# Ranks of the last batch and the second plan moved earlier, low halves ahead of the finish, and four banks for the products of the experts

## The reference

```python
x = x + xattn(layernorm(x), ctx, Wq, Wg, bg, Wkv, Wo)
# the second layer
y = layernorm(x)
w, sel = top_k(y @ Wr, 2); w = softmax(w)          # Wr: 512 x 8
gate = einsum('bsk,bske->bse', w, one_hot(sel, 8))
for e in range(8):
    out = out + gate[..., e:e+1] * (y @ We[e] + be[e])   # We[e]: 512 x 512
x = x + out
```

## Time and profile before

| | |
|---|---|
| median of 3 runs | 540.89 us |
| the profiled execution's own time | 540.51 us |
| its span | 538.5 us |
| TensorE busy | 517.9 us, 96% of the span |
| VectorE busy | 310.1 us |
| GpSimd busy | 213.4 us |
| adds of the second stage | 39, a median of 5.4 us (result buffers `khat`) and 5.5 us (`buf`) from issue to landing |

### The profile page before, as it was taken

How to read it: one execution, slowest core, us unless ns; L and a number is a source line. 1 busy time by engine, 2 the same in 40 slices (tenths; PEclk the granted TensorE clock), 3 DMA queues, 4 the chain that set the end, 5 groups by cost and what they waited for, 6 DMA issues and landing times.

```text
span 538.5 us, 12127 instructions
## 1 busy us (share of the span) xinstructions
PE 517.9 (96%) x4084; PEld 420.6 (78%) x4084; DVE 310.1 (58%) x918; ACT 209.2 (39%) x372; POOL 213.4 (40%) x238
## 2 busy tenths in 40 slices
PE   7999999999999999999999999999999988999992
PEld 4777788888878878887888888788887766888881
DVE  4583348647434773853467386366876777555551
ACT  5455432443433234344323434532253332344430
POOL 4451566412565033146601633100124663445453
PEclk9999999999999999999999999999999998999997
DMA  8922446981445117235420741398979996767765
GB/s 279 392 93 73 163 137 186 265 297 49 154 160 185 50 73 242 80 122 198 139 96 10 265 159 54 130 365 283 365 270 216 219 271 126 163 135 124 158 87 68
DMA packets 41242, 92.94 MB, mean 173 GB/s; under 512 B 5152, under 2 KB 5152, under 8 KB 41056
## 3 DMA queue, kind: packets, MB, share of 16 engines
q0 software_dynamic: 15184, 42.56, 29.9%
q1 hardware_dynamic: 25424, 48.58, 27.0%
q10 hardware_dynamic: 576, 1.05, 0.6%
HBM read 53.81 MB, written 40.18 MB: 175 GB/s over the span
## 4 chain that ended last, share of the span: by engine, by line
PE 78%; DMA 12%; DVE 3%; issue 3%; POOLq 2%; ACT 1%; POOL 0%; SPq 0%; DVEq 0%
PE pj L1173 22%; PE pj L1175 21%; PE pj L1174 21%; PE tp L1165 7%; DMA out_dram<-buf,out_idx 5%; DMA out_dram<-khat,out_idx 5%; PE pj L1260 3%; PE kvb L1232 2%; PE pj L1182 1%; DMA wraw<-in_L_xattn_Wkv_dram 1%; PE tp L1240 1%; POOLq L616 1%; POOLq L617 1%; ACT buf L702 0%; PE kvb L1165 0%
## 5 line engine op out<-in xcount | busy, mean ns | idle before, releaser
L1173 PE MATMUL pj<-R 128*128 128x512 f32 x448 | 183.6, 410 | 0.9 <-DVE R L821 0.9
L1175 PE MATMUL pj<-R 128*128 128x512 f32 x448 | 175.6, 392 | 0.0
L1174 PE MATMUL pj<-R 128*128 128x512 f32 x448 | 174.7, 390 | 0.0
L1173 PEld LDWEIGHTS pj<-R 128*128 128x128 f32 x448 | 84.3, 188 | 19.3 <-DVE R L830 2.2
L1175 PEld LDWEIGHTS pj<-R 128*128 128x128 f32 x448 | 84.1, 188 | 18.9
L1174 PEld LDWEIGHTS pj<-R 128*128 128x128 f32 x448 | 84.5, 189 | 15.0
L1173 PE MATMUL pj<-R,aux 128*128 x156 | 65.2, 418 | 4.9 <-DVE aux L834 3.5
L1175 PE MATMUL pj<-R,aux 128*128 x156 | 62.1, 398 | 0.0
L1174 PE MATMUL pj<-R,aux 128*128 x156 | 61.5, 394 | 0.0
L513 POOL TENSOR_TENSOR rstd<-rstd,mhalf 128x1 f32<-128x1 f32 (+1 forms) x20 | 13.3, 665 | 108.5 <-DVE rstd L848 108.5
L830 DVE TENSOR_TENSOR R<-tp,R 128x512 fp32r<-128x512 f32 x64 | 43.4, 683 | 14.5 <-ACT R L659 14.5
(11 more groups left out here) (197 smaller groups left out, 725.2 us busy)
## 6 DMA issues: line engine op xcount, KB each, us to landing
we_halves<-aux POOLq DMA_DIRECT2D x28, 512.0 KB, 4.7
R<-we_halves SPq DMA_DIRECT2D x28, 512.0 KB, 6.2
buf<-xs SPq DMA_DIRECT2D x39, 264.0 KB, 4.6
buf<-in_ctx_dram SPq DMA_DIRECT2D x15, 512.0 KB, 4.0
wraw<-in_L_ffn_We_dram POOLq DMA_DIRECT2D x14, 512.0 KB, 5.3
wraw<-in_x_dram SPq DMA_DIRECT2D x4, 1024.0 KB, 9.9
out_dram<-gate SPq DMA_DIRECT2D x3, 1024.0 KB, 5.2
xs<-zeros POOLq DMA_DIRECT2D x4, 594.0 KB, 9.1
```

Of the source, the lines that this page charges most:

```text
L1173: nc.tensor.matmul(bank[:, :], s_hi(k), m_hi(k), start=(k == 0), stop=False)
L1174: nc.tensor.matmul(bank[:, :], s_hi(k), m_lo(k), start=False, stop=False)
L1175: last = nc.tensor.matmul(bank[:, :], s_lo(k), m_hi(k), start=False, stop=(k == KT - 1))
```

## The change

1. `START` has L 3 ahead of tile 7 (it was behind it), K 2 behind tile 7 (was behind 8), K 3 behind tile 8 (was behind 10).
2. VectorE and ScalarE walk a second list, `LATE`, made of `START`: from tile 8 on the finish M of tile m stands behind T of tile m + 2. TensorE and GpSimd still walk `START`.
3. The product of tile m from 8 on goes to bank `pj[m % 4]`, and waits for the finish of m - 4 instead of m - 2; tiles 10 and 11 wait for the ranks of quarters 2 and 3 instead.
4. The six pieces of `plan_rest` stand one ahead of each finish of the tiles 9 to 14. The row starts (`tile_row`) are in the fifth piece and raise `planned` to 2, which SyncE waits for as before; the flags for the adds and the row masks are in the sixth and raise it to 3, for which VectorE and GpSimd wait. Three memsets of one element become one of three.

On TensorE, with bank numbers: the rows from the last matmul of tile 6 to the first of tile 7, before. Line 1191 is K 1, line 1182 would be an L, line 1240 the turn of tile 8.

The diff, cut to its core:

```diff
-        START += [("K", "", 1)] + tiles(7) + [("L", "", 3)] + tiles(8) + [("K", "", 2)] + tiles(9) + tiles(10) + [("K", "", 3)]
+        START += [("K", "", 1), ("L", "", 3)] + tiles(7) + [("K", "", 2)] + tiles(8) + [("K", "", 3)] + tiles(9) + tiles(10)
...
+        LATE, due = [], []
+        for place_ in START:
+            if place_[0] == "M" and place_[2] >= 8:
+                due.append(place_)
+                continue
+            LATE.append(place_)
+            if place_[:2] == ("T", "m"):
+                LATE += due
+                due = []
+        LATE += due
+
+        def m_bank(m):
+
+            return pj[m % (2 if m < 8 else 4)]
...
             for step, kind, i in START:
                 if step == "M":
                     if i == M0:
-                        pool.wait_ge(planned, 2)
+                        pool.wait_ge(planned, 3)
...
-            for step, kind, i in START:
+            for n, (step, kind, i) in enumerate(LATE):
                 if step == "T" and kind == "m":
-                    e_of = expert_of(i - 1)
+                    e_of = expert_of(LATE[n + 1][2]) if LATE[n + 1][0] == "M" else None
...
+                link(nc.vector.tensor_tensor(more, big, over(shift_e[:, :], M1), ALU.mult))
+                link(nc.vector.tensor_reduce(tile_o[:, :], more, AX_X, ALU.add))
+                link(nc.vector.tensor_tensor(tile_b[:, :], iota_t[:, :], tile_o[:, :], ALU.add))
+                flag_tiles(ends, bound, big, more, tile_u)
+                link(nc.vector.scalar_tensor_tensor(tile_u, tile_b[:, :], float(P), tile_u, ALU.mult, ALU.min))
+                nc.vector.scalar_tensor_tensor(tile_row[:, M0:M_ALL], tile_e[:, :], float(ROWS), tile_u, ALU.mult, ALU.add).then_inc(planned, 1)
+                yield
...
             planning = plan_rest(bias[:, :])
-            for step, kind, i in START:
+            for step, kind, i in LATE:
                 if step == "T" and kind == "m":
                     low_m(i, i % 2)
                     pay(i)
                 elif step == "M":
-                    if i >= 11:
-                        next(planning, None)
+                    if i >= 9:
                         next(planning, None)
                     copy_y(i)
...
-                pe.wait_ge(MOE["y_copied"], mth(m - 2))
+                if m in (10, 11):
+                    pe.wait_ge(SEMS["ranked"], nth("ranked", LAST, m - 8))
+                else:
+                    pe.wait_ge(MOE["y_copied"], mth(m - (2 if m < 10 else 4)))
...
-                three(pj[slot], lambda k: xsT_hi[:, slot, k, :], lambda k: xsT_lo[:, slot, k, :],
+                three(m_bank(m), lambda k: xsT_hi[:, slot, k, :], lambda k: xsT_lo[:, slot, k, :],
```

More of the change, by code:

```diff
@@ L791, in _ @@
                 elif step == "M":
-                    if i == M_ALL - 1:
-                        e_of = expert_of(i)
-                    gate_bias(i, e_of)
+                    gate_bias(i, expert_of(i) if e_of is None else e_of)
+                    e_of = None
                 elif step == "L":
@@ L1074, in plan_rest @@
                 halves_at(tmp, HALVES - 1, bound, last[:, 1:1 + E])
-                for zero in (last, flag, ends):
-                    link(nc.vector.memset(zero[:, 0:1], 0.0))
+                firsts = tmp[:, at + 3 * M1 + 2 * (E + 1):at + 3 * M1 + 5 * (E + 1)].rearrange("p (a e) -> p a e", a=3)
+                link(nc.vector.memset(firsts[:, :, 0:1], 0.0))
                 link(nc.vector.tensor_tensor(first, first, last[:, 0:E], ALU.is_ge))
@@ L1089, in plan_rest @@
                 yield
+                link(nc.vector.tensor_tensor(more, big, over(shift_e[:, :], M1), ALU.mult))
[5 more added lines that the diff above has]
+                yield
+                link(nc.vector.scalar_tensor_tensor(tile_o, tile_b[:, :], float(P), tile_u, ALU.mult, ALU.subtract))
+                nc.vector.scalar_tensor_tensor(taken[:, :], tile_o, lane[:, 0:1], zeros[:, TOKEN:TOKEN + 1].broadcast_to((P, M1)), ALU.is_gt, ALU.mult)
                 flag_tiles(flag, bound, big, more, tile_u)
@@ L1093, in plan_rest @@
                 nc.vector.tensor_tensor(tile_alone[:, M0:M_ALL], tile_u, offs[:, 2:3].broadcast_to((P, M1)), ALU.mult)
[L1094 to L1105, removed]
+                nc.vector.scalar_tensor_tensor(tile_early[:, M0:M_ALL], tile_t[:, :], 1.0, offs[:, 2:3].broadcast_to((P, M1)), ALU.is_le, ALU.mult).then_inc(planned, 1)
+                dve.wait_ge(planned, 3)
             dve.wait_ge(zeroed, 1)
@@ L1123, in copy_y @@
                 dve.wait_ge(bias_gated, m + 1)
-                nc.vector.scalar_tensor_tensor(y_sb[m % YS], pj[m % 2][:, :], w_sel[:, m % (2 * YS):m % (2 * YS) + 1], y_sb[m % YS],
+                nc.vector.scalar_tensor_tensor(y_sb[m % YS], m_bank(m)[:, :], w_sel[:, m % (2 * YS):m % (2 * YS) + 1], y_sb[m % YS],
                                                ALU.mult, ALU.add).then_inc(MOE["y_copied"], 1)
             planning = plan_rest(bias[:, :])
-            for step, kind, i in START:
+            for step, kind, i in LATE:
                 if step == "T" and kind == "m":
```

## The result

The changed kernel takes 543.68 us (median of 11 runs, 540.13 to 546.34) against 540.86 us (11 runs, 539.81 to 543.58) before: a ratio of 1.0043, interval 1.0023 to 1.0063. Two more sets of runs, each on a chip shared with its own runs of before, gave 1.0029 (1.0004 to 1.0055) and 1.0034 (1.0014 to 1.0053). So the change is slower, by 1.6 to 2.3 us by these ratios (the medians differ by 1.4 to 2.8). The forecast was 541.4, the range 539.0 to 543.6.

What follows compares the result with a forecast made beforehand. TensorE's time and GpSimd's queue of adds, close together, were taken to bound the kernel. The 540.51 us of before plus 0.85 for the later add of tile 30 gave 541.4 us; range 539.0 to 543.6.

Steps and rivals of the forecast that it cites:

- What bounds: Whole kernel: TensorE's time and GpSimd's queue of adds bound it, close together; TensorE's gains count only as adds follow.
- the chain at the end is still made of adds: Expected sign at the end of the run: the last chain of waits goes from add to add.
- an end of the adds that moves with TensorE: Sign at the end of the run that would show the forecast wrong.
- Ranks earlier: TensorE ahead of L 3: it waits for the ranks of quarter 1, so tile 11 turns 1.2 us later.
- The second plan: VectorE's planning pieces around tiles 11 to 14: row starts written at 448.15, only 1.6 us earlier than before.
- The wait in its place and the clock: TensorE ahead of tile 17: waits 3.3 to 4.5 us for the load, then loses 1.6 to low clock.
- The finish is later for the adds: VectorE at tile 30: its finish ends at 505.5 behind tile 32's low half, so add 30 is issued 0.85 us later.
- Other tiles before 30 have more room: GpSimd's adds before tile 30 wait for landings, not finishes, so later finishes were given no cost there.
- Rival A: Longer pause at tile 17 brings more than one half-clock stretch; tile 18 turns at 459.2; 543.0 us, chance 0.26.
- B: The clock holds through the pause at tile 17; TensorE gains 2.1 us; 539.8 us, chance 0.16.
- C: Tile 17's load comes early enough, TensorE stays dense and adds alone bound; 538.8 us, chance 0.08.
- D: Going round four banks with small pauses makes the clock fall repeatedly, costing 14 us; 555 us, chance 0.01.

Runs made afterwards that it cites:

- control 1: The changed kernel run again with no edit, on the chip of three of the experiments: 542.90 us, ratio 1.0029 to the kernel before.
- control 2: The changed kernel run once more with no edit, on the chip of three other experiments: 543.73 us, ratio 1.0034 to the kernel before.

## Why the prediction was right or wrong

**What bounds.** Right in that there are two bounds close together, and the runs without adds put 4.2 us on the adds. But "the chain at the end is still made of adds" holds in full for one of the three profiles of the changed kernel. In the other two the chain stays on TensorE to 518.8 and to 504.6, as "an end of the adds that moves with TensorE" would have it, which the prediction called a sign of being wrong.

**Ranks earlier.** Right. 1.12 us of pause ahead of L 3 came, and tile 11 turned 1.2 to 1.3 us later from tile 0 where I took 1.2.

**The second plan.** Right in place, too early in time. `tile_row` was forecast at 448.15, and came at 448.49 in a profile whose stage begins 0.73 earlier, so at 449.2 on my scale: 1.1 later than the sum. Of the 1.6 that it should have gained, 0.6 came. What I did not see is that the late list itself made it late. I took the position of the pieces as given and summed what VectorE does up to it; the run without the late list shows 445.54, 59.1 from the turn of tile 0 against 62.0 in the changed kernel.

**The wait in its place and the clock.** Right in kind: a pause released by the load, and a mean clock of 0.72 as forecast. The pause was 2.79, under the 3.3 to 4.5 forecast, as the load landed in 2.79 us, not 3.4. Tile 17 turned at 65.9 from tile 0, where I had 65.8 (452.8 - 387.0), and that is luck in part: row starts 1.1 later and a load 0.6 shorter work against each other. Tile 18 came within 0.1 us of before, where I had a gain of 0.5, and 0.3 to 0.7 later than before in the controls. The 2.79 is near the estimate of 2.6 from the fit for GpSimd's DMAs in the Trainium skill (DMA: Bandwidth & Descriptors, section Anatomy of one DMA); control 1 has 2.71, and one of the experiments 3.27.

**The finish is later for the adds.** The mechanism is there, and its size at tile 30 came out: the finish of tile 30 follows the payment and ends 1.8 later than before from tile 0, add 30 follows it by 1.08 and comes at 119.9, before at 118.9. That is 1.0 later, forecast 0.85. In the controls it is 1.8 later, and in control 1 add 30 follows its finish by 1.08 too:

```profile
503.42 0.69 DVE L848 TENSOR_TENSOR aux<-tp,aux 128x512 fp32r<-128x512 f32 x1 [1.58 <-ACT aux L761]
...
504.25 0.15 DVE L991 TENSOR_TENSOR out_idx<-taken,buf 128x1 uint32<-128x1 f32 x1
504.32 0.75 DVE L1138 SCALAR_TENSOR_TENSOR buf<-pj,w_sel,buf 128x512 f32<-128x512 f32 x1
```

What failed is the next step, that this is the only delay: "Other tiles before 30 have more room: their adds wait for landings, not for finishes". Before, no add from tile 8 on follows its finish by less than 1.5 us. In the first profile of the changed kernel those of tiles 8, 16 and 27 to 30 follow it by 1.05 to 1.3. Add 8 came 2.2 to 3.7 us later, behind its late finish there and behind the earlier scatters in the controls. Add 16 followed its finish by 1.29 (460.19 to 461.48) and came 0.5 to 1.5 later than before. Add 17, which must wait for the landing of 16, came 1.3 to 2.4 later. In the kernels without a pause at tile 17 it came 0.1 to 1.0 later. I put all of this at nothing. How much of it reaches the end is not shown: in the first profile the delay of add 17 is down to 0.2 at add 22.

**Sum and rivals.** 541.4 was 2.3 under the measured median; against before the forecast was +0.5 and the sets show +1.4 to +2.8. Counted from the turn of tile 0 to the end of the span, the three profiles show +0.3, +2.0 and +3.2, where the sum had +0.85. The first median, 543.68, lies 0.08 above the range of 539.0 to 543.6, control 1 (542.90) inside it and control 2 (543.73) 0.13 above. The band "within 0.3%", to which I gave 0.56, was missed by the first set (0.43%) and control 2 (0.34%); control 1 (0.29%) lies just inside it. Rival A has the nearest number (543.0), but not for its reason: all three profiles have a single stretch of low clock behind the pause, and tile 18 turns 0.1 earlier to 0.7 later than before, where A had 1.1 later. So A is not shown as the cause. B (no low clock) was made by hand with zeros and gave 1.4 us, not clear of nothing. C was made several times: without the pause the time was mostly within 0.3% of before, where C had -1.7 us. C took add 13 to hang on its finish. With the plan one tile earlier that finish ended 1.6 us earlier, and add 13 came 1.8 later, at 67.0 from tile 0, since the adds from tile 9 on already follow one another's landings. D did not happen: the clock from 458 to 528 is 1.00 in the first profile.

## What to carry to other kernels

When work is pinned to a step of a list (here the planner's pieces to the finishes), moving the step moves the work; check what each moved step carries before asking what it frees. When a second queue runs within a few us of the dense engine, list for every link of it, from the first, what it waits for and by how much that comes last; a link that has room before the change may have none after it. And where two causes hold the same event, undoing either alone does not move it: add 8 came back only when late list and early scatters both went.

## What the runs showed of the hardware

- Pauses of TensorE of 2.1 to 3.3 us, in nine profiles, were followed by matmuls at 1.2 GHz (mean granted clock 0.72 over 6 us); behind the pause of 1.12 ahead of L 3 the clock stayed at 1.00, and so it did with products of zeros for 2.74 us of the wait.
- Behind TensorE's last matmul the granted clock fell too, to 0.50 from 535 to 538, so the mean clock of an execution also tells how long the rest went on.
- An accumulating indirect DMA of 128 rows of 2 KB takes GpSimd 1.54 to 1.65 us to issue and lands 3.1 to 8.4 us later (before and the changed kernel). The standard deviation of the time of the kernel before was 1.1 to 2.0 us by set with these adds and 0.7 without them.
- The same kernel had a median of 541.4, 542.3 and 545.3 us on the chips of the three sets of experiments; without adds 541.1 on the last of these. Only ratios within a set compare.
